# One ACT queue, two copies swapped: the output's transpose is evicted ahead of the squares of Q

## The reference, cut to what matters

```
def attn_layer(x, Wqkv, qs, ksc, Wo):        # 16 heads of 64, windows of 32 rows
    q, k, v = jnp.split(x @ Wqkv, 3, -1)      # each 512 x 1024 for one batch
    ...
    q = l2norm(q) * qs
    k = l2norm(k) * ksc
    q = q * cos * scale + rotate_half(q) * sin * scale
    k = k * cos * inv + rotate_half(k) * sin * inv
    out = local_attention(q, k, v)            # each window sees itself and the one before
    return out.transpose(0, 2, 1, 3).reshape(b, n, INNER) @ Wo

for i in range(6):
    x = attn_layer(shift_tokens(x), ...) + x
    x = ffn_layer(shift_tokens(x), ...) + x
```

## Time and profile before

| | before |
|---|---|
| time, median of 3 runs | 5536.82 us (5531.36 to 5545.69) |
| the profiled execution: its time, its span | 5534.48 us, 5532.5 us |
| mean granted TensorE clock, share of 2.4 GHz | 0.907 |
| busy PE | 4490.3 us (81%) |
| busy DVE | 3605.5 us (65%) |
| busy POOL | 2513.4 us (45%) |
| busy ACT | 2432.7 us (44%) |

### The profile page before, as it was taken

One profiled execution on the slowest core, in us unless ns is written; L12 is line 12 of the kernel. 1 busy time (PEld: TensorE's weight loads), 2 busy tenths in 40 slices (PEclk: granted clock), 3 DMA queues, 4 the chain that ended last, 5 costly groups with the idle time before them and its releaser, 6 DMA issues. The chain is left out here.

```text
span 5532.5 us, 169536 instructions
## 1 busy us (share of the span) xinstructions
PE 4490.3 (81%) x70369; PEld 2832.7 (51%) x70369; DVE 3605.5 (65%) x6107; ACT 2432.7 (44%) x3020; POOL 2513.4 (45%) x3540
## 2 busy tenths in 40 slices
PE   3555666777679998899988999799988999889997
PEld 2333323222226665566655666466665666556664
DVE  6665566665557776677756777576766777567774
ACT  2433433344344444444434444354444454444453
POOL 2000011111137674477626767176653777356771
PEclk9888877788789999999999999899999999999998
DMA  0000000000012222122212222122221222122220
GB/s 27 0 0 0 0 1 0 0 0 0 0 36 68 73 73 56 46 68 69 71 37 65 69 72 71 29 75 69 68 66 38 69 73 71 40 61 70 71 74 16
DMA packets 156862, 247.95 MB, mean 45 GB/s; under 512 B 33488, under 2 KB 50896, under 8 KB 155472
## 3 DMA queue, kind: packets, MB, share of 16 engines
q1 hardware_dynamic: 156240, 238.09, 16.3%
HBM read 20.38 MB, written 2.10 MB: 4 GB/s over the span
## 5 line engine op out<-in xcount | busy, mean ns | idle before, releaser
L1085 ACT ACTIVATE ls_r<-PS 128x1024 f32<-128x1024 f32 x192 | 196.5, 1023 | 1054.8 <-PE PS L963 1054.8
L1164 DVE TENSOR_TENSOR ls_a<-PS,TC 128x1024 f32<-128x1024 f32 x384 | 467.5, 1219 | 171.2 <-ACT ls_r L1085 170.8
L866 POOL TENSOR_TENSOR ls_a<-ls_a,ls_q 128x1024 f32<-128x1024 f32 x192 | 452.9, 2359 | 263.6 <-DVE ls_q L1169 263.6
L1174 DVE TENSOR_REDUCE ls_ss<-ls_r 128x16 f32<-128x1024 f32 x384 | 466.2, 1214 | 86.0 <-ACT ls_r L1110 86.0
L1169 DVE TENSOR_TENSOR ls_q<-PS,TS 128x512 f32<-128x512 f32 x768 | 491.0, 680 | 0.0
L381 POOL TENSOR_TENSOR QT<-MXT,ONE 3x512 bf16<-3x512 bf16 x128 | 146.9, 1148 | 732.7 <-ACT MXT L534 725.5
L886 POOL TENSOR_TENSOR ls_a<-ls_a,ls_q 128x1024 f32<-128x1024 f32 x192 | 455.2, 2371 | 0.0
L963 PE MATMUL PS<-WQ,ls_xsT 128*128 128x512 f32 x768 | 438.8, 700 | 18.4 <-issue 9.7
L1020 PE MATMUL PS<-WO,ls_r 128*128 128x128 f32 x3072 | 404.3, 286 | 58.9 <-ACT ls_r L1113 58.9
L1181 DVE TENSOR_REDUCE ls_mx<-PS 128x8 f32<-128x512 f32 x384 | 263.0, 685 | 246.2 <-PE PS L948 246.2
L1020 PEld LDWEIGHTS PS<-WO,ls_r 128*128 128x128 f32 x3072 | 367.1, 196 | 105.6 <-ACT ls_r L1113 105.6
(11 more groups left out here) (217 smaller groups left out, 9128.2 us busy)
## 6 DMA issues: line engine op xcount, KB each, us to landing
ls_vb<-ls_vt SPq DMA_DIRECT2D x1152, 130.0 KB
ls_vb<-ls_vt SPq DMA_DIRECT2D x672, 65.0 KB
ls_xs<-XL SPq DMA_DIRECT2D x42, 256.0 KB, 2.4
WQ<-wqkv SPq DMA_DIRECT2D x6, 1536.0 KB, 6.5
ls_vb<-ls_vz SPq DMA_DIRECT2D x96, 65.0 KB
WO<-wo SPq DMA_DIRECT2D x24, 128.0 KB, 6.2
X<-x SPq DMA_DIRECT2D x8, 256.0 KB, 5.2
out<-X SPq DMA_DIRECT2D x8, 256.0 KB, 3.5
```

The lines of the kernel that those rows point to most:

```text
L866: pool.tensor_tensor(a4[:, 1], a4[:, 1], b4[:, 1], ALU.add).then_inc(s_ck, 1)
L1164: nc.vector.tensor_tensor(v4(A[fq])[:, a], src, tab, ALU.mult).then_inc(done, 1)
L1174: nc.vector.tensor_reduce(ss[:, fq, a * H:a * H + H], v4(SQ)[:, a], AX.X, ALU.add).then_inc(done, 1)
```

## The change

In each slot ACT now copies Y^T of the back tile out of PSUM before it squares Q of the front tile. Both keep their waits and their signals, and no other engine's queue is touched. In slots that have no front, or no back, nothing changes; 30 of the 32 squares of a layer have a copy beside them.

```
@@ -1103,14 +1103,14 @@
                             act.wait_ge(s_kt, nm)
                             k0 = WIN + mt * P
                             act.activation(kT[:, :, k0:k0 + P], banks(KT_BANK, 2).rearrange("p (i n) -> p i n", n=P), ACT.Copy).then_inc(s_kte, 1)
+                        if back:
+                            act.wait_ge(s_yt, n)
+                            act.activation(YT, banks(Y_BANK, 2), ACT.Copy).then_inc(s_yte, 1)
                         if front:
                             act.wait_ge(s_q, nf)
                             if order > 1:
                                 act.wait_ge(s_rdq, nf - 1)
                             act.activation(SQ[:, 0:INNER], banks(Q_BANK, 2), ACT.Square).then_inc(s_sqq, 1)
-                        if back:
-                            act.wait_ge(s_yt, n)
-                            act.activation(YT, banks(Y_BANK, 2), ACT.Copy).then_inc(s_yte, 1)
                         if mid:
                             act.wait_ge(s_qt, nm)
                             act.activation(qT[:, :, :].rearrange("p i n -> p (i n)"), banks(QT_BANK, 2), ACT.Copy).then_inc(s_qte, 1)
```

## The result

The changed kernel takes 5607.8 us (median of 4 runs, 5604.5 to 5627.2), the kernel before 5534.1 (4 runs, 5526.6 to 5545.7). The ratio, which is that of the means, is 1.0139, 95% interval 1.0109 to 1.0168: 77 us slower (74 by the medians). The forecast was 5601, 65 us slower.

The account below looks back on a forecast made before the run. Two nearly equal rings bound it: PE's (values product round to itself) and DVE's (squares, norms, rotations, L997). 5534.5 + 65 (loop 55.9, after it 3.6, draining 5.6) = 5599.6; half of 2.3 on top gives 5601 us, range 5562 to 5650.

Parts of the forecast that it names:

- The delay itself: On ACT after the swap: Y^T copy 0.05 us earlier, squares of Q 1.78 later, Q^T copy 0.88 later.
- Slack along DVE's chain: DVE, norms to L997: waits plus overlap absorb 1.06 (slot 0-1) and 1.17 us (2-3), leaving 0.72 and 0.61.
- Slot 1-2: Slot with next batch's row transposes on PE: slack 1.55 plus 0.23 before L997 absorbs all 1.78 us; nothing left.
- if slot 1-2 grew: Sign of being wrong: slot 1-2 was to stay at 15.6 us.
- Jump: Slot 3 to the next pass's 0: DVE idles 4.76 us before L1181 and 2.10 before L1164; nothing left.
- if the jump slots' clock changed: Sign of being wrong: the slot between passes was to stay the same.
- Draining and last slots: After the loop: 3.6 us for two slots with a front tile, 5.6 for the first draining slot, over six layers.
- no slack from overlap: Three DVE waits absorb only their idle time; 5633 us, chance 0.12.
- PE pays as well: Late Q^T copy, POOL's L883 and K product delay PE, 0.2 to 0.35 us a slot more; 5635 to 5660, chance 0.14.
- PE's three near misses: Q^T copy, POOL's L883 and the K product each come within 0.25 us of delaying PE.
- nothing arrives: Waits undervalued by 0.6 us a slot swallow DVE's delay; 5527 to 5537 us, no change, chance 0.07.
- the clock gives it back: Jumps between passes escape the low clock, 2.83 us each, 102 us if all; faster from 29 jumps on, chance 0.04.

Follow-up runs that it names:

- the doses: Kernel before, ACT's order untouched, one or two extra DVE sums ahead of Q's norms (0.79 or 1.58 us late): 5540.5 and 5599.9 us.
- 2.70 late: Changed kernel with the squares of Q moved behind the Q^T copy as well: 5778.7 us, ratio 1.0434.
- the small dose: Kernel before, one extra DVE sum ahead of Q's norms, making them 0.79 us late: 5540.5 us, ratio 0.9997.
- the repaired kernel: Changed kernel with DVE's sines of Q moved ahead of both norms, into its wait for the squares: 5596.5 us, ratio 1.0092.
- the halved copy: Kernel before, Y^T copied in two halves, each with a signal; the output product's first chunks wait for the first alone: 5496.2 us, ratio 0.9906.

## Why the prediction was right

- *The delay itself.* 0.05 earlier for the copy, 1.78 later for the squares, 0.88 for Q^T: as in the rows after, to 0.02 (0.06, 1.78 to 1.80, 0.87).
- *Slack along DVE's chain.* The step that carried the sum. Counting each wait's idle time plus 0.08 for the overlap that a waiting instruction forgoes gave 1.06 and 1.17; the doses show 1.12 and 1.23. Left over were 0.66 and 0.55 us a slot, forecast 0.72 and 0.61. Most of the gap is the choice of slots, not the count: the three that were read take 14.89, 15.61 and 14.99 us, the means are 14.93, 15.68 and 15.04, and against 13.81 (14.02 in 1-2) those very slots have 1.08, 1.59 and 1.18 of slack.
- *Slot 1-2: the one step that failed.* I took the 0.23 us between K's sines and L997 for slack. It isn't. The same interval stands in the changed kernel, where DVE is what PE waits for:

```profile
2438.39 1.28 DVE L1169 TENSOR_TENSOR ls_q<-PS,TS 128x512 f32<-128x512 f32 x2
...
2439.95 1.35 PEld L997 LDWEIGHTS PS<-ls_vb,ls_q 64*32 64x32 f32 x128 [0.44 <-issue]
```

2439.95 - 2439.67 = 0.28, and 0.28 is the mean of all 42 in every kernel here, with the norms on time or 2.70 late, where slots 0-1 and 2-3 have 0.07 after. It is a longer handover in this slot; why wasn't tried. Without the 0.23 the count is 1.55, against the 1.59 that this slot has. It cost 5 us, and it is one of the signs of being wrong that the prediction named ("if slot 1-2 grew").
- *Jump.* The idle microseconds took the delay in: jumps with 6.8 us at 1.2 GHz take 21.72 before, 21.39 in the changed kernel, and 21.75 and 21.72 with the norms 1.58 and 2.70 late. The mean rose by 0.13 all the same, because 35 of 36 jumps now hold 6.8 us of the low clock instead of 26. That is the prediction's other sign ("if the jump slots' clock changed"). The mix alone would have cost 16 us (35 x 21.72 + 20.65, less the 764 of before); the 0.33 by which the like ones were shorter took 12 of them back, and isn't explained.
- *Draining and last slots.* Mis-sized, 13.0 us instead of 9.2. About 1 us of this is a draining slot that held no time at 1.2 GHz before and 3.4 us after.
- *Rival "no slack from overlap".* Fell. By it the small dose would cost nothing either, but 1.58 would cost 1.58 - 0.76 - 0.06 = 0.76 in slots 0-1 and 0.65 in 2-3; measured are 0.46 and 0.35. With it falls the rule as I took it from the Trainium skill, VectorE: DVE Perf Modes, "The DRAIN you can't avoid". I had left out that the same section lets a next instruction that isn't held start earlier; the sums of 1.21 us that start 1.12 apart agree with that.
- *Rival "PE pays as well".* In slots 0-1 and 2-3, none of it: with ACT's order and Q^T untouched, 1.58 us of late norms gave the same ring plus lateness, and from the norms to L997 DVE has no idle time left in which PE or POOL could have held it. PE's three near misses are real (0.05, 0.05, 0.21), and the repaired kernel pays for POOL's.
- *Rival "nothing arrives".* Fell with the result. It holds for 0.79 us late, as the small dose shows; by the slack, up to 1.1.
- *Rival "the clock gives it back".* Didn't come; the jumps met the low clock more often, not less. Whether the edit caused that isn't shown: the halved copy, with shorter passes, met it more as well, and 17 executions of the kernel before had mean granted clocks from 0.900 (5562 us) to 0.908 (5523 us) without any edit.

## What to carry to other kernels

Moving an instruction ahead in an in-order queue makes all that it passes wait for its semaphore: price the passed ones by how late they become, not by the idle time of their engine, 56% of the span here. Then follow the late result around its ring and subtract each wait on the way (plus the overlap that waiting instructions forgo) until something is left or nothing. A ring that doesn't bind swallows up to its slack and then charges one for one; so first find which ring binds, and shorten that one: 0.4 us out of PE's ring gave 0.9%, and the same edit gave nothing once DVE's ring was the longer.

## What the runs showed of the hardware that I had not expected

- The length of slots 2-3 followed max(15.04, 13.81 + lateness) within about 0.01 us over lateness from 0.79 to 2.70 us. The handover from DVE's sines to PE's L997 is as constant: 0.07 us in the 84 slots 0-1 and 2-3 of the changed kernel, but 0.28 in its 42 slots 1-2.
- Two sums over 1024 columns (1.21 us each) without a wait between them started 1.12 us apart.
- Jump slots fell into three classes by the time at 1.2 GHz in them, 18.9, 20.7 and 21.7 us, with none, 3.4 and 6.8 us of it, in the kernel before. The mix moved from 4/6/26 to 0/1/35 in the changed kernel's profiled execution, where the last class took 21.4.
- With PE waiting 2.27 us for one copy in each slot, 3.4 us at 1.2 GHz appeared in 26 of 126 ordinary slots, at 1.3 to 1.7 us each; with 0.52 us of that wait in none.
